# Software-pipelined block sums, moved DMA issues and a reordered chunk loop in a Householder-scan layer on eight cores

## The reference

```python
xz = x @ Win.T;  xi, z = split(xz)                 # 1024 -> 2 x 2048
log_lam = -8 * softplus(omega) * sigmoid(xi @ Wl.T + bl);  lam = exp(log_lam)
v = xi @ Wv.T + bv
# over time: h_0 = xi_0, then
vh, vv = sum(v_t * h), sum(v_t * v_t)
Qh = h - 2 * v_t * (vh / vv)                       # Householder step
h = lam_t * Qh + (1 - lam_t) * x_t
y = layernorm(x + (silu(z) * h) @ Wout.T)
x_int = clip(round(y / scale), -127, 127)
out = layernorm(y + (x_int * scale) @ (ternary - 1).T + b_ffn)
```

## Time and profile before

| | us |
|---|---|
| median of 3 runs | 2698.22 (2696.32 to 2972.57) |
| the profiled execution | 2698.97 |
| span of its slowest core (core 2) | 2697.4 |
| spans of the eight cores | 2673.3 to 2697.4 |
| TensorE busy on core 2 | 2443.2 (91%) |
| VectorE, ScalarE busy | 1554.4 (58%), 716.3 (27%) |
| mean DMA rate | 216 GB/s |

### The profile page before, as it was taken

One profiled execution on the slowest core, in us unless ns is written; L12 is line 12 of the kernel. 1 busy time (PEld: TensorE's weight loads), 2 busy tenths in 40 slices (PEclk: granted clock), 3 DMA queues, 4 the chain that ended last, 5 costly groups with the idle time before them and its releaser, 6 DMA issues.

```text
span 2697.4 us, 33024 instructions; the slowest of 8 cores (2673.3 to 2697.4 us)
## 1 busy us (share of the span) xinstructions
PE 2443.2 (91%) x11504; PEld 1450.4 (54%) x11504; DVE 1554.4 (58%) x2039; ACT 716.3 (27%) x1004; POOL 0.2 (0%) x4
## 2 busy tenths in 40 slices
PE   8986787799999899999999699999998879999997
PEld 6875566577785344444443244444444555555553
DVE  6555555555540555455556155556554767777776
ACT  4333333343330222212122122122222111111111
POOL 0000000000000000000000000000000000000000
PEclk9998888899999899999999799999999989999998
DMA  6766666799988666776678977676656976666650
GB/s 187 217 201 205 202 227 199 234 247 267 242 226 256 199 202 202 233 234 206 186 220 265 266 225 212 190 210 207 210 181 224 313 256 204 210 210 219 218 188 32
DMA packets 383300, 582.19 MB, mean 216 GB/s; under 512 B 17312, under 2 KB 271776, under 8 KB 368032
## 3 DMA queue, kind: packets, MB, share of 16 engines
q1 hardware_dynamic: 383136, 580.09, 69.3%
HBM read 355.62 MB, written 224.40 MB: 215 GB/s over the span
## 4 chain that ended last, share of the span: by engine, by line
PE 41%; DVE 21%; DMA 12%; SPq 12%; ACT 8%; issue 6%; DVEq 1%; ACTq 0%
PE pb L179 40%; SPq L197 11%; DVE CO L200 5%; ACT CO L194 4%; DVE TS L200 4%; DMA xcs<-CO 3%; DVE W L200 3%; DVE W L793 2%; DMA WC<-wcs 2%; DMA GRAW<-w_v 1%; DMA ORAW<-w_out 1%; DMA ORAW<-w_ffn 1%; DVE GPS L646 1%; DVE GRE L643 1%; DVE GV L200 1%
## 5 line engine op out<-in xcount | busy, mean ns | idle before, releaser
L179 PE MATMUL pb<-XC,WC 128*128 128x512 bf16 x5376 | 1182.2, 383 | 68.6 <-DMA WC<-wcs 50.6
L179 PEld LDWEIGHTS pb<-XC,WC 128*128 128x128 bf16 x5376 | 528.3, 99 | 718.6 <-issue 102.0
L179 PE MATMUL pb<-XH,WH 128*128 128x512 f32 x1024 | 285.2, 401 | 117.0 <-ACT WH L194 104.6
L179 PE MATMUL pb<-WO,GHL 128*128 128x512 bf16 x1536 | 359.2, 380 | 3.6 <-ACT STT L194 3.0
L200 DVE TENSOR_TENSOR CO<-TS,CO 128x512 bf16<-128x512 f32 (+1 forms) x200 | 159.9, 799 | 222.6 <-ACT CO L194 222.6
L179 PEld LDWEIGHTS pb<-XH,WH 128*128 128x128 f32 x1024 | 196.6, 193 | 164.2 <-issue 123.9
L179 PE MATMUL pb<-XL,WH 128*128 128x512 f32 x1024 | 282.7, 399 | 0.0
L179 PE MATMUL pb<-XH,WL 128*128 128x512 f32 x1024 | 278.9, 395 | 0.0
L194 ACT ACTIVATE CO<-TS 128x512 bf16<-128x512 f32 (+1 forms) x200 | 143.3, 716 | 373.7 <-DVE TS L200 373.7
L179 PEld LDWEIGHTS pb<-WO,GHL 128*128 128x128 bf16 x1536 | 150.0, 98 | 153.2 <-issue 6.0
L179 PEld LDWEIGHTS pb<-XL,WH 128*128 128x128 f32 x1024 | 198.3, 194 | 42.4
(11 more groups left out here) (105 smaller groups left out, 1974.7 us busy)
## 6 DMA issues: line engine op xcount, KB each, us to landing
WC<-wcs SPq DMA_DIRECT2D x224, 512.0 KB, 7.1
wcs<-CO SPq DMA_DIRECT2D x224, 256.0 KB, 3.9
xcs<-CO SPq DMA_DIRECT2D x56, 512.0 KB, 3.6
XC<-xcs SPq DMA_DIRECT2D x28, 1024.0 KB, 16.4
xfs<-XF SPq DMA_DIRECT2D x16, 1024.0 KB, 9.1
GRAW<-w_l SPq DMA_DIRECT2D x32, 512.0 KB, 7.3
GRAW<-w_v SPq DMA_DIRECT2D x32, 512.0 KB, 7.7
zs<-ZOUT SPq DMA_DIRECT2D x16, 1024.0 KB, 11.8
```

What stands on the lines that cost most here:

```text
L179: return q.do("tensor", lambda e: e.matmul(out, lhsT, rhs, start=start, stop=stop), waits, inc)
```

## The change

Six edits, none of which changes what is computed.

1. `sums` defers the low part: the sum and the high part of product m are issued before the low part and the store of product m-1.
2. In the projection loop `sums_w` and `more_loads` come ahead of `sums_x`, and `more_loads` is called from p = 2 on.
3. The first three WC loads and the load of XC0 (`early`) are issued before the last but one `mm_in`'s matmuls are written (p = 30); for that the sixth WC buffer's place becomes the third, and the waits of the first six WC loads are split.
4. `prep` is cut into `prep_load` (m = 6 of the quad before), `prep_split` (m = 4) and `prep_store` (m = 2 of the next one); quads 15 and 16 have none, so the jobs run to quad 27. The stores of `values` (`put_values`) are issued in the next quad, at m = 1 and 3. `load_xn` goes to m = 4 and 5.
5. The banks of the last quad's products are 1 + m % 5 instead of m % 6, its chain steps run from m = 3, ic = 4 to m = 5, ic = 2, and `gamma`, `scan(0)` at m = 5, ic = 4 instead of m = 6, ic = 2.
6. In the chunk loop `mm_ffn(c-2)` stands ahead of `gram(c+1)` and `chain_prep(c+1)`.

```diff
-    WC_KB = [144.25, 148.25, 152.25, 156.25, 160.25, 188.25]
+    WC_KB = [144.25, 148.25, 188.25, 152.25, 156.25, 160.25]
...
+        todo = []
+
+        def lower():
+            m, src, out, hi, lo, t_h, tw, old, sem, r = todo.pop(0)
+            t_l = tt(lo, src, hi, AL.subtract, (t_h,) + tw + old)
+            if r is not None:
+                t_ts[r] = (t_h, t_l)
+            k = int(sem[2:])
+            t_co[k:k + width] = [store(m, out, sem, (t_h, t_l))] * width
+            last.extend((t_h, t_l))
...
             t_h = act(hi, src, AF.Copy, tw + old)
-            t_l = tt(lo, src, hi, AL.subtract, (t_h,) + tw + old)
-            if b is not None:
-                t_ts[r] = (t_h, t_l)
-            t_s = store(m, out, "co%d" % k, (t_h, t_l))
-            t_co[k:k + width] = [t_s] * width
-            last += [t_h, t_l]
+
+            if todo:
+                lower()
+            todo.append((m, src, out, hi, lo, t_h, tw, old, "co%d" % k, r))
+        lower()
         return tuple(last)
...
     def bank(qi, m):
-        return (7 * qi + m) % 8 if qi < NQ - 1 else m % 6
+        return (7 * qi + m) % 8 if qi < NQ - 1 else 1 + m % 5
...
+    def early():
+
+        for g in range(3):
+            load_wc(g)
+        load_xc(0, 0, 0)
+        load_xc(0, 0, 1)
...
-        if p <= NIC and p % 2 == 0:
-            more_loads(p)
-            sums_x(p // 2 - 1)
         for _ in range(WAT.get(p, 0)):
             more_loads(p)
             sums_w(wdone, BUFS[wdone])
             wdone += 1
-        if p >= 3:
+        if p >= 2:
             more_loads(p)
+        if p <= NIC and p % 2 == 0:
+            sums_x(p // 2 - 1)
+        if p == 2 * NIC - 2:
+            early()
...
-        if (m == 4 and ic in (2, 4, 6)) or (m == 5 and ic in (0, 2, 4, 6)) or (m == 6 and ic == 0):
-            chain_step({4: ic // 2 - 1, 5: 3 + ic // 2, 6: 7}[m])
-        if m == 6 and ic == 2:
+        at = 8 * m + ic - 28
+        if 0 <= at < 16 and at % 2 == 0:
+            chain_step(at // 2)
+        if at == 16:
             gamma(0)
             scan(0)
...
-            if m == 2 and 2 <= qi < 2 + NIC + NDC:
-                prep(qi - 2, (t_in_pe,) + t_gr_free[1] if qi == 2 else ())
-            if m == 3 and kind == 0:
-                load_xn(qi, 0)
-                load_xn(qi, 1)
+            k = PREP.get(qi)
+            if k is not None and m == 2:
+                if k:
+                    prep_store(k - 1)
+                else:
+                    prep_load(0, (t_in_pe,) + t_gr_free[1])
+            if k is not None and m == 4:
+                prep_split(k, (t_in_pe,) + t_gr_free[1] if k == 0 else ())
+            if k is not None and m == 6 and k + 1 < NIC + NDC:
+                prep_load(k + 1)
...
+            if kind == 0 and qi and m in (1, 3):
+                put_values(qi - 1, m // 2)
+            if kind == 0 and m >= 4 and m < 6:
+                load_xn(qi, m - 4)
...
+        if 0 <= c - 2 < NCH:
+            mm_ffn(c - 2)
         if ahead:
             gram(c + 1)
             chain_prep(c + 1)
-        if 0 <= c - 2 < NCH:
-            mm_ffn(c - 2)
```

More of the change, by code:

```diff
@@ L422, in build @@
[L422 to L457, removed]
@@ L525, in load_wc @@
         if g < RING:
-            ws = tuple(t_co) + (t_wh[2 * NIC - 1, 1], t_wl[2 * NIC - 1, 1]) + t_gr_free[1]
+            ws = (tuple(t_co) if g < 2 else t_gr_free[1] if g == 2 else
+                  (t_wh[2 * NIC - 1, 1], t_wl[2 * NIC - 1, 1]))
         else:
@@ new lines, in build @@
+    t_con = dma(CSL2[:, :], c_sl2[:, :], "lc")
+    split_w(0, 0)
+    split_x(0)
+    split_w(1, 0)
+    split_w(0, 1)
+    split_w(1, 1)
+    for dc in range(NDC):
+        if dc:
+            split_x(dc)
+        if dc + 2 < NDC:
+            load_x(dc + 2)
+        for ec in range(2):
+            t_wmm[ec] = mm_in(ec, dc)
+        if dc == 3:
+            load_w(2)
+            load_w(3)
+    t_e = act(WOM2[:, :], WOM, AF.Exp, (t_con,))
+    t_e = act(WOM2[:, :], WOM2[:, :], AF.Ln, (t_e,), bias=1.0)
@@ new lines, in build @@
+    t_e = dve(lambda e: e.tensor_scalar_mul(WOM2[:, :], WOM2[:, :], -8.0), (t_e,))
+    t_wom = dve(lambda e: e.tensor_scalar_mul(WOMN[:, :], WOM2[:, :], -1.0), (t_e,))
+    t_c = dve(lambda e: e.tensor_copy(IDB[:, :], IDE[:, :]), (t_con,))
+    t_c = dve(lambda e: e.tensor_scalar_max(SCL[:, :], SCL[:, :], 1e-5), (t_con,))
+    t_con2 = dve(lambda e: e.reciprocal(RSC[:, :], SCL[:, :]), (t_c,))
+    WAT = {p: 2 if 16 < p < 26 and p % 2 else 1 for p in range(3, 30)}
+    BUFS = [0 if n < 14 else n % 2 for n in range(32)]
@@ new lines, in build, with more_loads @@
+    wdone = 0
+    def more_loads(p):
+        nonlocal wload
+        while wload < min(32, wdone + 2):
+            b = BUFS[wload]
+            if b in BUFS[wdone:wload] or (b and p <= NIC):
+                break
+            load_sums_w(wload, b)
+            wload += 1
+    wload = 0
+    split_w(2)
+    evac_in(0)
+    for p in range(2, 2 * NIC):
+        evac_in(p - 1)
+        if p + 1 < 2 * NIC:
+            split_w(p + 1)
+        if p + 2 < 2 * NIC:
+            load_w(p + 2)
+        for _ in range(WAT.get(p, 0)):
+            more_loads(p)
+            sums_w(wdone, BUFS[wdone])
+            wdone += 1
+        if p >= 2:
+            more_loads(p)
+        if p <= NIC and p % 2 == 0:
+            sums_x(p // 2 - 1)
+        if p == 2 * NIC - 2:
+            early()
+        t_dc = []
+        for dc in range(NDC):
+            t_wmm[p] = mm_in(p, dc)
+            t_dc.append(t_wmm[p])
@@ L921, in second_norm @@
         return first, second, stats, last
-    for g in range(RING):
+    for g in range(3, RING):
         load_wc(g)
-    for m in range(7):
+    for m in range(1, 7):
         for part in range(2):
@@ L951, in last_hooks @@
             chain_prep(0)
-        if (m == 4 and ic in (2, 4, 6)) or (m == 5 and ic in (0, 2, 4, 6)) or (m == 6 and ic == 0):
-            chain_step({4: ic // 2 - 1, 5: 3 + ic // 2, 6: 7}[m])
-        if m == 6 and ic == 2:
+        at = 8 * m + ic - 28
+        if 0 <= at < 16 and at % 2 == 0:
+            chain_step(at // 2)
+        if at == 16:
             gamma(0)
             scan(0)
+    PREP = {qi: k for k, qi in enumerate([qi for qi in range(2, 28) if qi not in (15, 16)])}
     for qi, (h, jc, kind) in enumerate(QUADS):
```

99 lines of the change are left out of this document (47 added, 52 removed).

## The result

| | before | after |
|---|---|---|
| median (lowest to highest) of 4 runs, us | 2699.69 (2696.32 to 2972.57) | 2547.12 (2539.63 to 2830.04) |
| ratio of after to before | | 0.943, 95% interval 0.9385 to 0.9474 |
| the profiled execution | 2698.97 | 2539.63 |
| span of core 2 | 2697.4 | 2536.0 |

The change makes the kernel 5.7% faster, some 153 us, where the forecast was 205 us and a time of 2493 us in a range of 2465 to 2540. The direction was right; the median lies 7 us above the range.

What follows compares the result with a forecast made beforehand. TensorE was taken as the bound, paced by another engine in the projections' first half. Terms of 114.3 + 11.7 + 48 + 7.4 + 17 + 7 = 205 us gave 2493 us, range 2465 to 2540.

Steps and rivals of the forecast that it cites:

- The sums: First half of the projections: deferred low parts and reordered sums let TensorE fill the pairs, 114.3 us won.
- The prediction's own signs: Projections: VectorE's wait for CO under 30 us, TensorE's for WH under 15, pairs of 43.7 us.
- the second half: Second half of the projections: it keeps its loss of 10.8 us, since TensorE is nearly full there.
- The DMAs bound the projections: Projections, first rival: DMA cost per byte sets 47.7 us a pair, 26 us lost, time 2519; 20%.
- First loads: Start of the gates: earlier WC and XC loads win 11.7 us, about 7 us of wait remain before product 6.
- The gates' DMAs: Gates after product 6: moved loads and stores win 48 of 54.4 us lost, 3 us of stops left.
- The third rival: Gates, XC reload: it still stops TensorE, half of the 41 us stay, time 2513; 10%.
- The last quad: Last gates quad: gram gains 3.8 us and waits about 10, scan(0) and what follows start 7.4 us earlier.
- The feed-forward and its clock: Chunk loop: a shorter wait wins 17 us over 13 chunks, and the clock gives 7 us back.
- The chunk loop's rival: Chunk loop: it gains nothing since VectorE sets it; 24 us stay if the first chain step waits too, 2517; 10%.
- The sums stay as slow: Projections, rival: TS ring or CO slots keep VectorE waiting, half of 114 us stays, time 2550; 4%.
- The denser TensorE: Projections and gates, rival: dense matmuls are granted a lower clock, taking back 205 us, time over 2700; 2%.

Runs made afterwards that it cites:

- Run 10: Changed kernel with every second of the first fourteen GRAW loads left out, all projection products kept; 2518.2 us in one execution, pairs of 43.4 us.
- runs 8 to 10: Changed kernel: 8, no WL x XH product, fewer GRAW loads, 39.6 us a pair; 9, no such product, half of xcs stores, 45.7; 10, fewer GRAW loads, 43.4.
- Experiments 2 and 12: Changed kernel: 2, ns store first, xi loads at m = 2, 4, 2609.8 us; 12, also GRAW halves, GpSimd memset, no Wout in quads 14-17, 2524.0 us.
- experiment 3: Changed kernel with mm_ffn put back behind gram and chain_prep; 2624.6 and 2629.1 us.
- the first group: Follow-up runs 1 to 4, made on a chip with another clock, where the kernel before takes 2726.8 to 2736.6 us.
- experiment 1: Changed kernel with every second of the first fourteen GRAW loads replaced by an HBM copy nobody waits for; 2606.0 us, ratio 0.9542.

## Why the prediction was wrong, point by point

**The sums (114.3 forecast for the first half, 87.2 measured): the step that failed.** "Moving `sums_w` and its GRAW load ahead of `sums_x` puts the x set over the load's landing, so that wait goes too." It did not go. A pair has two GRAW loads and one x set, and the x set can cover one of them. In the kernel before it covered one already: ScalarE waited for GRAW once a pair, 45.5 us in 7 waits on core 2, at the w set of the iteration without an x set. Edit 2 only changed which of the two is covered; after has 53.0 us in 7. The exposed one is issued when the w set of one iteration ends and is awaited by the w set of the next, with only a split between (issued at 248.97, there at 258.6). So about a quarter of VectorE's 181.2 us in the earlier trace rows was this load and not the ping-pong. I counted VectorE's work per pair (33 us, right: 207.7 of 308.3 us are 32.9 of 48.8) and compared it with 43.7 us, "with 10 to spare", without laying the chain out once with both loads in it: 33 and a wait of 9.1 are 42, and the small waits for ScalarE and the CO slots, 7 us more, take it over. Run 10 shows the whole term: without the exposed load the pairs take 43.4 us. The prediction's own signs failed with it: VectorE waited 96 us for CO, not under 30, and the pair took 48.8 us. What remained of the deferral was right: 119 waits for CO became 50, the TS ring held, and the second half even gained 7.6 us that I had left out (3.2 lost instead of 10.8, at a share of 0.99).

**The rival that was near the right number by luck.** "The DMAs bound the projections" forecast 47.7 us a pair, and 48.8 came. Its mechanism is refuted by runs 8 to 10: 288 GB/s are moved when the chain lets them, and dropping 14% of the bytes leaves the pair within 0.7 us. Its time, 2519, was also too low, because the other terms fell short too. As to the price per byte "0.89 for 239 GB/s": the second half after moves 260 GB/s at 0.99, so the share per byte was about that, but in the first half, which set the pair, 258 GB/s cost only 0.83.

**First loads (11.7; measured 12.1).** Right, with the wait where it was put: 7.93 us before product 6, where 7 were forecast.

**The gates' DMAs (48; measured 40.1).** No WC wait in ordinary pairs: the 2657 matmuls from 784.70 to 1360 fill 575.23 of 575.30 us. The reload is the mis-sized term: 13 us lost instead of 3. SyncE of after, core 2, from quad 15's first XC load on:

```profile
1305.06 1.87 SPq L197 DMA_DIRECT2D XC<-xcs  x2
...
1353.13 3.10 SPq L197 DMA_DIRECT2D XC<-xcs  x2
1356.33 4.86 SPq L197 DMA_DIRECT2D WC<-wcs  x2
1361.28 0.63 SPq L197 DMA_DIRECT2D ks<-GGE  x1
1362.00 5.43 SPq L197 DMA_DIRECT2D as_<-GRE  x1
...
1390.48 2.33 SPq L197 DMA_DIRECT2D ss<-GLS  x1
```

A step with one WC and two XC loads takes (1353.13 - 1305.06) / 6 = 8.0 us, the forecast's 8. Then the ten value stores and the two WC loads between them take from 1361.28 to 1392.8, 31.5 us, where I had 8 to 9 us for five stores, the price in an ordinary pair (1284.62 to 1295.5 is 10.9). Behind a queue with 60 us of reload in it, the two sets cost 16.4 and 12.5. "That is on the edge" was the right reading; 3 us was not the right price for an edge. The third rival, half of 41 us stay, was too high by 7.

**The last quad (3.8 and 3.6; measured -1.4 and -4.4).** Gram(0) waited 14.89 us instead of 10. VectorE's `forget` of quad 30 stood for an xi load that the prediction had called covered ("`forget` and `load_xn`, which wait for them, come 15 us later"):

```profile
1900.04 1.22 DVE L578 SCALAR_TENSOR_TENSOR GNC<-GLS,GNC 128x1024 f32<-128x1024 f32 x1 [10.95 <-DMA GNC<-xfs]
...
1924.20 0.07 DVE L1024 MEMSET A<- 128x16 f32 x1
```

`load_xn` now stands at m = 4 and 5, behind ten value stores that SyncE issues until 1888.67, so it goes out at 1890.78. In the 16 forget quads VectorE waits 162.2 us for these loads, which it did not before; in 15 of them the banks of the next products cover it, in the last one STATE does not. Experiments 2 and 12 shorten the wait by 5 and 11 us. After gram(0) nothing is won. I take it that the loads of WO and of the feed-forward's weights set the pace there: from the first WO load to gram(3) it is 105.3 us before and 107.3 after, and an earlier chain buys nothing when its transfers don't land earlier. No run takes these loads away, so this is not shown.

**The feed-forward and its clock (24; measured 20.1, in experiment 3 by 17 to 21).** The periods are 33.49 us, and the wait is 0.89 for GHL instead of 2.03 for STATE, at a clock of 0.99. The forecast had 33.4 and 0.7. The chunk loop's rival falls.

**The rest.** "The sums stay as slow" falls with the waits. The denser TensorE got no lower clock on the chip of the prediction: the granted clock is 1.00 for 575 and 473 us on end. On another chip the clock was lower, see below.

## What to carry to other kernels

When a producer chain is pipelined to hide one latency, write out its period once as a serial list of work and of every transfer that is issued and awaited inside it: a busy sum with "10 us to spare" says nothing of a load with one buffer whose issue and use are neighbours. When a rival's number fits, it is not yet its mechanism: take away the wait and the bytes separately, and don't keep the bytes with a copy of another kind. A transfer moved behind others is priced by what stands ahead of it at that place, not by its price in a quiet one, and a ring that hides returning stores should not be spent for another buffer.

## What the runs showed of the hardware that was not expected

Granted clocks differ between chips, and between kinds of matmul on one chip. On the chip of the first group TensorE never stops in the projections and is yet slower; experiment 1, 22 to 147, 150 to 300 and 900 to 1300 us:

```profile
22.00:147.00 125.00, 125.00 (x493) 103.46 (x494) 74.76 (x76) 50.54 (x63) 0.00 (x0) 0.86 0.70 214
```

```profile
150.00:300.00 150.00, 150.00 (x583) 124.46 (x582) 100.59 (x123) 65.71 (x95) 0.00 (x0) 0.84 0.87 255
...
900.00:1300.00 400.00, 400.00 (x1851) 181.23 (x1850) 218.56 (x275) 107.51 (x119) 0.00 (x0) 1.00 0.81 220
```

Its fp32r projections have a mean granted clock of 0.84 to 0.86 with 0.253 to 0.257 us a matmul, where the earlier trace rows has 1.00 and 0.2275; its bf16 gates run at 1.00 and 0.216 us as on the other chips. TensorE had not idled in either stretch, so this is not a clock that comes back after a stop. The mean mixes two paces, as shorter windows of the same core show:

```profile
190.00:210.00 20.00, 20.00 (x78) 16.60 (x77) 12.35 (x17) 8.26 (x13) 0.00 (x0) 0.81 0.81 254
211.00:217.00 6.00, 6.00 (x28) 4.96 (x27) 2.94 (x4) 4.31 (x8) 0.00 (x0) 0.97 0.97 199
217.00:260.00 43.00, 43.00 (x166) 35.72 (x165) 30.15 (x37) 17.39 (x24) 0.00 (x0) 0.81 0.87 265
```

For some 43 of each 50 us the granted clock is 0.81, between the two levels, and four matmuls take 1.05 us; then, once a pair, it is back near 1.00 for about 6 us and four take 0.91. What lets it come back there, and why the gates are spared, no run shows. Nor is it shown that a denser TensorE brings it on: the kernel before has a lower mean clock on this chip too (0.92 to 0.94, where it has 0.957 on core 2 of the first profile).

The rule of the Trainium skill ("TensorE: Matmul & The Clock Gate", Part 1) is that a die with three or more cores at dense matmuls goes to 13/16, which is 0.8125. The 0.81 of these stretches agrees. Two things do not: an estimate by that rule is 0.2275 x 16/13 = 0.280 us for the projections' matmul, and it took 1.05 / 4 = 0.2625; and the rule would hold in the gates too, which ran at 1.00. In run 10, on another chip, TensorE is dense at a granted clock of 1.00 in both stages, from 150 to 430 us and from 790 to 1340 us.
